# Splitting an FFN activation at half its value, and moving one sigmoid: a sixteen-group transformer-like block on one Trainium2 core

## The chip, the cores and the metric

The kernel runs on one NeuronCore of a Trainium2 chip. Five engines work side by side, each through its own list of instructions in order, and wait for one another on semaphores: TensorE (PE in the rows, its weight loads PEld), VectorE (DVE), ScalarE (ACT), GpSimd (POOL) and SyncE (SP), which only issues transfers here. The metric is the device time of one execution in microseconds (us), lower being better. Kernel before: 286.07 us, median of three runs (285.97 to 286.13).

## The reference, cut to what matters

The input is 32 x 256 rows of 128 numbers. Three layers follow each other, each added to its input:

```
x = x + 0.5 * ffn(layernorm(x))      # first FFN
x = x + rnn(layernorm(x))            # gated recurrence along the 256 steps
x = x + 0.5 * ffn(layernorm(x))      # second FFN, the same weights

ffn(x): h = gelu(ternary_linear(x, w_up))      # 128 -> 512
        return ternary_linear(h, w_down)       # 512 -> 128
ternary_linear(x, w): w_t = sign(w) where |w| > 0.5 * mean|w|, else 0
        rms = sqrt(sum(x*x)) / sqrt(d)
        return (x / (rms + 1e-8)) @ w_t.T
rnn(x): f = sigmoid(x Wf), i = sigmoid(x Wi), c = max(x Wh + 0.5, sigmoid(x Wh))
        hidden_t = f_t * hidden_(t-1) + i_t * c_t,  hidden_0 = 0.5
```

(The recurrence is written in logarithms in the reference; this is what it comes to.) The second linear layer of the FFN divides by the root mean square of h itself, so the kernel needs the sum of squares of each row's 512 values of h, beside h times w_down.

## The kernel before, in words

The 8192 rows stay in SBUF as tensor X, 64 tiles of 128 rows; four tiles are a group, and there are 16 groups. The program passes three times over the groups: 16 steps of the first FFN (F = 0 to 15), 16 steps of the recurrence (r = 0 to 15), 16 steps of the second FFN (F = 16 to 31). Each engine has its own hand-written order of these steps; they overlap only as far as those orders and the semaphores let them.

One step of the FFN, for group F:

- GpSimd normalises the group's four tiles (norm, L213, writes xn) two steps ahead, and turns sums of squares into root mean squares (rms_step, L220 and L224). It also computes the square roots of the layer norms (ln_roots, L187 to L195): in the second FFN one group's roots in each step up to step 11.
- TensorE: up(F, 0) (L405, L406) multiplies the high and low fp16 halves of the transposed input with the ternary weights into PSUM tensor U[0]; turn transposes the next group (L386); up(F, 1) fills U[1]; gram(F-1) (L426, L434) forms h times h-transposed in blocks of 64 rows, whose diagonal holds the sums of squares; down(F-1) (L447) multiplies h with down_w.
- ScalarE: GeLU in place on U[0] (L294), the high half of the next transposed input (xt_hi, L275), h_hi = fp16 of a multiple of the GeLU (L300), the same GeLU and h_hi for U[1], then the diagonal's sums (sum_squares, L326).
- VectorE: the low half of the next input (xt_lo, L563); h_lo (L568), the rest of h that fp16 h_hi doesn't hold, once for U[0] and once for U[1]; then, for the group of two steps ago, y_scale (L583) and the addition into X (L590, four tiles); and layer norm statistics (L546, L552, L626) of groups to come.

up(F, part) waits for h_lo of the same part of group F-1, because both use U[part]. So per step there is one loop through TensorE, ScalarE and VectorE, and each of the four engines also has the sum of its own work.

h is kept as two fp16 tensors. Before, h_hi = fp16(256 h) and h_lo = fp16(256 h - h_hi). The first FFN's gram takes three products, hi x hi, hi x lo and lo x hi, 96 matmuls of 64 columns. The second FFN's gram takes two, hi x (hi/2) and hi x lo, 64 matmuls, for which VectorE writes a third tensor, h_half = h_hi / 2 (h_halves, L578), after each h_lo; gram waits for it.

One step r of the recurrence: TensorE transposes the next group, forms three gates (L462), and transposes the previous hidden state back (L471). ScalarE copies the transposed input (L306), makes sig_h (gate 0), sig_i (gate 1) and the forget gate (gate 2), all on L313, and normalises two of the four tiles of the group after next (norm_tile, L289), one before and one after sig_i. VectorE: scan (L608), candidate (L598, writes cand), statistics, addition (L614). GpSimd: inject = sig_i x cand (L232), then rstd and shift for a coming group (L200, L203), then the other two of the four tiles (L213). norm_tile waits for shift.

The functions that the change touches, and what calls them:

Of the kernel before, what the change touches and what calls it, by code (L numbers as in the profile page):

```python
# [12 lines left out]
P = 128  # L13
TILES = 4
GT = TILES * P
LN_EPS = 1e-5
RMS_EPS = 1e-8
H_SPLIT = 256.0
XN_SPLIT = 4096.0
POOL_TILES = 2  # L20
HALF = P // 2
# [3 lines left out]
def build_macaron(nc, x_in, w_f, w_i, w_h, w_up, w_down, x_out):  # L25
# [12 lines left out]
    with ExitStack() as ctx:  # L38
        def sb(name, shape, dt=F32):
            return ctx.enter_context(nc.sbuf_tensor(name, shape, dt))  # L40

        def sem(name):
            return ctx.enter_context(nc.semaphore(name))
# [31 lines left out]
        xt_lo = sb("xt_lo", [P, 2, GT], F16)  # L75
        h_hi = sb("h_hi", [P, 2, chunks, GT], F16)
        h_lo = sb("h_lo", [P, 2, chunks, GT], F16)
        h_half = sb("h_half", [P, 2, chunks, GT], F16)
        square_junk = sb("square_junk", [P, 2, TILES, P], BF16)
        ssq = sb("ssq", [P, 2, TILES])  # L80
        rms = sb("rms", [P, 2, TILES])
# [35 lines left out]
        shift_done, xn_act_ready = sem("shift_done"), sem("xn_act_ready")  # L117
        xn_ready, xt_ready, xt_taken, hi_ready = sem("xn_ready"), sem("xt_ready"), sem("xt_taken"), sem("hi_ready")
        up_ready, gelu_done = sem("up_ready"), sem("gelu_done")
        h_hi_done, h_lo_done, h_half_done = sem("h_hi_done"), sem("h_lo_done"), sem("h_half_done")  # L120
# [22 lines left out]
        def by_both(n):  # L143
            return groups + 2 <= n < 2 * groups
# [17 lines left out]
        def _(pool):  # L162
# [54 lines left out]
            def rms_step(F):  # L217
                par = F % 2
                pool.wait_ge(ssq_done, F + 1)
                eng.tensor_tensor(rms[:, par, :], ssq[:, par, :], half[:, 0:TILES], ALU.pow).then_inc(rms_ready, 1)  # L220
                pool.wait_ge(rms_ready, F + 1)


                eng.tensor_scalar(rms_den[:, F % 4, :], rms[:, par, :], 2.0 * ((1.0 if F < groups else 2.0) / dff) ** 0.5, 2.0 * H_SPLIT * RMS_EPS,  # L224
                                  ALU.mult, ALU.add).then_inc(rms_den_done, 1)

            def inject_step(g):
# [34 lines left out]
        def _(act):  # L262
# [88 lines left out]
            for r in range(groups):  # L351
                turned(groups + r + 1)
                gate(r, 0)
                if by_both(groups + r + 2):
                    norm_tile(groups + r + 2, 2)
                gate(r, 1)
                if by_both(groups + r + 2):
                    norm_tile(groups + r + 2, 3)
                gate(r, 2)
                if r == 0:  # L360
                    sum_squares(groups - 1)
                if r + 4 < groups:
                    rnn_moments(r + 4)
# [6 lines left out]
        def _(pe):  # L370
# [38 lines left out]
            def gram(F):  # L409

                par = F % 2
                pe.wait_ge(h_lo_done, 2 * F + 2)
                if F >= groups:
                    pe.wait_ge(h_half_done, 2 * (F - groups) + 2)
                if F == 0:
                    pe.wait_ge(consts_set, 5)
                    pe.wait_ge(mask_done, 2)
                    pe.wait_ge(w_taken, 2)  # L420
                elif F == groups:
                    pe.wait_ge(rnn_added, groups)
                if F >= 1:
                    pe.wait_ge(ssq_done, F)
                for n in range(2):
                    pe.matmul(G[n * HALF:(n + 1) * HALF, :, 0:HALF], ident16[:, n * HALF:(n + 1) * HALF], off_diag[:],  # L426
                              start=True, stop=False, tile_position=(0, n * HALF))
                for t in range(TILES):
                    for c in range(chunks):
                        last = t == TILES - 1 and c == chunks - 1  # L430
                        for left, right in ((h_hi, h_hi), (h_hi, h_lo), (h_lo, h_hi)) if F < groups else ((h_hi, h_half), (h_hi, h_lo)):
                            for n in range(2):
                                i = slice(t * P + n * HALF, t * P + (n + 1) * HALF)
                                m = pe.matmul(G[n * HALF:(n + 1) * HALF, t, 0:HALF], left[:, par, c, i], right[:, par, c, i],  # L434
                                              start=False, stop=last and (left is h_lo if F < groups else right is h_lo), tile_position=(0, n * HALF))
                m.then_inc(gram_done, 1)

            def down(F):
                par = F % 2
                if F == 0:  # L440
                    pe.wait_ge(w_taken, 3)
                if F >= 2:
                    pe.wait_ge(ffn_added, F - 1)
                for t in range(TILES):
                    for c in range(chunks):
                        for part in (h_hi, h_lo):
                            m = pe.matmul(Y[:, par, t, :], part[:, par, c, t * P:(t + 1) * P], down_w[:, c, :],  # L447
                                          start=(c == 0 and part is h_hi), stop=(c == chunks - 1 and part is h_lo))
                m.then_inc(down_done, 1)

# [65 lines left out]
        def _(dve):  # L516
# [48 lines left out]

            def h_low(F, part):
                dve.wait_ge(h_hi_done, 2 * F + part + 1)
                vec.scalar_tensor_tensor(out=h_lo[:, F % 2, 2 * part:2 * part + 2, :], in0=U[part][:], scalar=H_SPLIT,  # L568
                                         in1=h_hi[:, F % 2, 2 * part:2 * part + 2, :],
                                         op0=ALU.mult, op1=ALU.subtract).then_inc(h_lo_done, 1)  # L570

            def h_halves(F, part):
                if F < groups:
                    return
                dve.wait_ge(h_hi_done, 2 * F + part + 1)
                if F >= groups + 2:
                    dve.wait_ge(gram_done, F - 1)
                vec.tensor_scalar(h_half[:, F % 2, 2 * part:2 * part + 2, :], h_hi[:, F % 2, 2 * part:2 * part + 2, :],  # L578
                                  0.5, None, ALU.mult).then_inc(h_half_done, 1)

            def scale_y(F):
                dve.wait_ge(rms_den_done, F + 1)
# [73 lines left out]
            for s in range(0, 3 * groups + 2):  # L656
# [48 lines left out]
```

## Time and profile before

| | us |
|---|---|
| time, median of three runs | 286.07 |
| time of the profiled execution | 285.95 |
| its span, first to last instruction | 284.1 |
| outside the span | 1.85 |

| engine | busy us | share of the span |
|---|---|---|
| PE | 249.9 | 88% |
| DVE | 244.6 | 86% |
| ACT | 222.4 | 78% |
| POOL | 220.5 | 78% |

The busy times are sums over the three passes and a start and an end. Which engine holds a pass back is not told by them: for that one reads the chain of waits, stretch by stretch, and the rows of the engines in time order. In a timeline row the first number is the start, the second the length in us; a bracket at the end says how long the engine idled before the row, and what it waited for. Rows of several instructions give the time from the first start to the last end. Instructions of one engine overlap a little, so the distance from start to start is what one costs in a full stretch.

### The profile page before, as it was taken

The page shows a single profiled execution, that of the slowest core. Times are in us where ns is not written, and L with a number is a line of the kernel's source. Part 1 is how long each engine was busy: PE and PEld are TensorE (multiplying, and loading weights), DVE is VectorE, ACT ScalarE, POOL GpSimd, SP SyncE. Part 2 cuts the span into 40 slices and gives each one's busy share as a digit, 9 for nine tenths or more (in the row PEclk, how much of TensorE's full clock was granted, in tenths as well). Part 3 has the DMA queues.
Part 4 walks back from the last instruction along what each step waited for, and adds up shares of the span by engine and source line. Part 5 has one row for each costly group of instructions (what it writes and reads, how often), then busy time and mean ns, then how long its engine had stood idle before and what let it go on. Part 6 is the DMA issues. An engine that isn't in the chain of part 4 may idle for free.

```text
span 284.1 us, 10821 instructions
## 1 busy us (share of the span) xinstructions
PE 249.9 (88%) x4269; PEld 176.1 (62%) x4269; DVE 244.6 (86%) x772; ACT 222.4 (78%) x546; POOL 220.5 (78%) x394
## 2 busy tenths in 40 slices
PE   0568999999999999989999965668999999999973
PEld 0335877878778877735555533336777777667853
DVE  3767699999999898989999946678799999998894
ACT  1267789889898998778888863568999999998971
POOL 4888587878778756579888897898889999899231
PEclk9997999999999999999999999889999999999998
DMA  6990000000000000000000000000021112112213
GB/s 175 278 240 2 3 3 5 2 5 3 2 2 6 2 3 5 3 0 1 3 0 0 0 1 1 2 1 2 2 76 39 42 54 63 40 39 59 59 39 113
DMA packets 18051, 9.81 MB, mean 35 GB/s; under 512 B 592, under 2 KB 17872, under 8 KB 18000
## 3 DMA queue, kind: packets, MB, share of 16 engines
q1 hardware_dynamic: 16896, 8.39, 10.7%
q10 hardware_dynamic: 1104, 0.72, 0.9%
q8 instruction: 34, 0.56, 0.8%
q14 instruction: 17, 0.14, 0.2%
HBM read 4.92 MB, written 4.19 MB: 32 GB/s over the span
## 4 chain that ended last, share of the span: by engine, by line
POOL 38%; PE 37%; DVE 10%; issue 8%; ACT 4%; DMA 1%; POOLq 0%; DVEq 0%; ACTq 0%
PE Y L447 11%; POOL root L192 9%; PE G L434 9%; POOL xn L213 9%; POOL inject L232 6%; PE U L405 6%; PE U L406 5%; POOL rms L220 4%; POOL rstd L200 4%; PE T L386 3%; ACT h_hi L300 2%; ACT U L294 2%; PE G L426 2%; DVE X L590 1%; POOL den L195 1%
## 5 line engine op out<-in xcount | busy, mean ns | idle before, releaser
L294 ACT ACTIVATE U<-U 128x1024 f32<-128x1024 f32 x64 | 65.5, 1024 | 25.0 <-PE U L406 24.8
L568 DVE SCALAR_TENSOR_TENSOR h_lo<-U,h_hi 128x1024 f16<-128x1024 f32 x64 | 77.3, 1218 | 7.3 <-ACT h_hi L300 6.9
L213 POOL TENSOR_SCALAR xn<-X,neg_mean,rstd 128x128 f32<-128x128 f32 x164 | 74.2, 467 | 7.2 <-DVE rstd L559 5.0
L300 ACT ACTIVATE h_hi<-U 128x1024 f16<-128x1024 f32 x64 | 65.7, 1026 | 1.1
L447 PE MATMUL Y<-down_w,h_lo 128*128 128x128 f16 x512 | 60.8, 219 | 0.6 <-issue 0.6
L447 PE MATMUL Y<-down_w,h_hi 128*128 128x128 f16 x512 | 61.2, 220 | 0.0
L405 PE MATMUL U<-xt_hi,up_w 128*128 128x512 f16 x128 | 50.8, 397 | 5.4 <-DVE h_lo L568 4.1
L220 POOL TENSOR_TENSOR rms<-ssq,half 128x4 f32<-128x4 f32 x32 | 32.8, 1024 | 25.2 <-ACT square_junk L326 25.2
L192 POOL TENSOR_TENSOR root<-mv,half 128x8 f32<-128x8 f32 (+1 forms) x26 | 50.5, 1942 | 2.2
L406 PE MATMUL U<-xt_lo,up_w 128*128 128x512 f16 x128 | 50.8, 397 | 0.0
L447 PEld LDWEIGHTS Y<-down_w,h_lo 128*128 128x128 f16 x512 | 50.1, 98 | 0.9 <-issue 0.9
L447 PEld LDWEIGHTS Y<-down_w,h_hi 128*128 128x128 f16 x512 | 49.3, 98 | 1.3
L434 PE MATMUL G<-h_lo,h_hi 128*64 128x64 f16 x1024 | 44.6, 196 | 0.3 <-issue 0.3
L434 PEld LDWEIGHTS G<-h_lo,h_hi 128*64 128x64 f16 x1024 | 41.7, 113 | 0.0
L590 DVE SCALAR_TENSOR_TENSOR X<-Y,y_scale,X 128x128 f32<-128x128 f32 x128 | 36.0, 345 | 1.1
L386 PE MATMUL T<-ident,xn 128*128 128x128 f32 x192 | 31.0, 287 | 2.3 <-POOL xn L213 1.9
L386 PEld LDWEIGHTS T<-ident,xn 128*128 128x128 f32 x192 | 23.8, 148 | 12.9 <-POOL xn L213 4.8
L462 PE MATMUL U<-xt,gate_w 128*128 128x512 f32 x64 | 30.2, 594 | 0.0
L626 DVE BATCH_NORM_STATS2 st<-X 128x6 f32<-128x128 f32 x128 | 29.6, 276 | 0.0
L326 ACT ACTIVATE square_junk<-G 128x64 bf16<-128x64 f32 x128 | 26.7, 230 | 3.1 <-PE G L434 3.1
L232 POOL TENSOR_TENSOR inject<-sig_i,cand 128x512 f32<-128x512 f32 x16 | 20.4, 1274 | 9.2 <-DVE cand L598 6.3
L326 ACT ACTIVATION_READ_ACCUMULATOR square_junk<-G 128x1 f32 x128 | 26.2, 216 | 0.0
(75 smaller groups left out, 482.8 us busy)
## 6 DMA issues: line engine op xcount, KB each, us to landing
X<-in_L_attn_x SPq DMA_DIRECT2D x16, 256.0 KB, 5.2
out_x<-X SPq DMA_DIRECT2D x16, 256.0 KB, 2.5
up_raw<-in_L_ffn_w_up ACTq DMA_DIRECT2D x1, 256.0 KB, 4.1
down_raw<-in_L_ffn_w_down ACTq DMA_DIRECT2D x1, 256.0 KB, 5.0
gate_raw<-in_L_attn_Wh ACTq DMA_DIRECT2D x1, 64.0 KB, 4.5
gate_raw<-in_L_attn_Wi ACTq DMA_DIRECT2D x1, 64.0 KB, 4.3
gate_raw<-in_L_attn_Wf ACTq DMA_DIRECT2D x1, 64.0 KB, 4.2
```

Of the source, the lines that this page charges most:

```text
L192: eng.tensor_tensor(root[l][:, par, 0:w, :], mv[l][:, cols(first, w), 1:3], half[:, 0:2 * w].rearrange("p (t e) -> p t e", e=2), ALU.pow). ...
L213: m = eng.tensor_scalar(xn[:, n % 2, t, :], X[:, c, :], neg_mean[l][:, c:c + 1], rstd[l][:, c:c + 1], ALU.add, ALU.mult)
L220: eng.tensor_tensor(rms[:, par, :], ssq[:, par, :], half[:, 0:TILES], ALU.pow).then_inc(rms_ready, 1)
L294: eng.activation(U[part][:], U[part][:], ACT.Gelu, scale=1.0 / XN_SPLIT).then_inc(gelu_done, 1)
L300: eng.mul(h_hi[:, F % 2, 2 * part:2 * part + 2, :], U[part][:], H_SPLIT).then_inc(h_hi_done, 1)
L326: m = eng.activation(square_junk[:, F % 2, t, 0:HALF], G[:, t, 0:HALF], ACT.Relu, accum_out=ssq[:, F % 2, t:t + 1])
L386: m = pe.transpose(T[:, t * P:(t + 1) * P], xn[:, n % 2, t, :], ident[:])
L405: pe.matmul(U[part][:, c, :], up_w[:, f0:f0 + P], xt_hi[:, F % 2, :], start=True, stop=False)
L406: m = pe.matmul(U[part][:, c, :], up_w[:, f0:f0 + P], xt_lo[:, F % 2, :], start=False, stop=True)
L434: m = pe.matmul(G[n * HALF:(n + 1) * HALF, t, 0:HALF], left[:, par, c, i], right[:, par, c, i], start=False, stop=last and (left is h_lo i ...
L447: m = pe.matmul(Y[:, par, t, :], part[:, par, c, t * P:(t + 1) * P], down_w[:, c, :], start=(c == 0 and part is h_hi), stop=(c == chunks - ...
L568: vec.scalar_tensor_tensor(out=h_lo[:, F % 2, 2 * part:2 * part + 2, :], in0=U[part][:], scalar=H_SPLIT, in1=h_hi[:, F % 2, 2 * part:2 * p ...
```

## The change

Three edits.

- h_hi becomes fp16(h / 2) and h_lo = fp16(h - 2 h_hi). As (h/2)^2 is h_hi^2 + h_hi h_lo but for the square of half the rest, both FFNs' gram takes two products, hi x hi and hi x lo, and h_half and its waits are gone. In return down needs h_hi x w + h_lo x (w/2): a second copy of the weights, down_w_half, is written once by VectorE in step 1, and down(0) waits for it.
- h_lo is written with its operands the other way round: first operand h_hi (fp16, SBUF), second U (fp32, PSUM).
- In the recurrence ScalarE makes sig_i before both tiles that it normalises, not between them.

```diff
-H_SPLIT = 256.0
+H_SPLIT = 0.5
...
             for r in range(groups):
                 turned(groups + r + 1)
                 gate(r, 0)
+                gate(r, 1)
                 if by_both(groups + r + 2):
                     norm_tile(groups + r + 2, 2)
-                gate(r, 1)
-                if by_both(groups + r + 2):
                     norm_tile(groups + r + 2, 3)
                 gate(r, 2)
...
                 pe.wait_ge(h_lo_done, 2 * F + 2)
-                if F >= groups:
-                    pe.wait_ge(h_half_done, 2 * (F - groups) + 2)
...
-                        for left, right in ((h_hi, h_hi), (h_hi, h_lo), (h_lo, h_hi)) if F < groups else ((h_hi, h_half), (h_hi, h_lo)):
+                        for right in (h_hi, h_lo):
...
             def down(F):
                 par = F % 2
                 if F == 0:
-                    pe.wait_ge(w_taken, 3)
+                    pe.wait_ge(w_halved, 1)
...
-                        for part in (h_hi, h_lo):
-                            m = pe.matmul(Y[:, par, t, :], part[:, par, c, t * P:(t + 1) * P], down_w[:, c, :],
+                        for part, w in ((h_hi, down_w), (h_lo, down_w_half)):
+                            m = pe.matmul(Y[:, par, t, :], part[:, par, c, t * P:(t + 1) * P], w[:, c, :],
...
-                vec.scalar_tensor_tensor(out=h_lo[:, F % 2, 2 * part:2 * part + 2, :], in0=U[part][:], scalar=H_SPLIT,
-                                         in1=h_hi[:, F % 2, 2 * part:2 * part + 2, :],
-                                         op0=ALU.mult, op1=ALU.subtract).then_inc(h_lo_done, 1)
...
-                vec.tensor_scalar(h_half[:, F % 2, 2 * part:2 * part + 2, :], h_hi[:, F % 2, 2 * part:2 * part + 2, :],
-                                  0.5, None, ALU.mult).then_inc(h_half_done, 1)
+                vec.scalar_tensor_tensor(out=h_lo[:, F % 2, 2 * part:2 * part + 2, :], in0=h_hi[:, F % 2, 2 * part:2 * part + 2, :],
+                                         scalar=-1.0 / H_SPLIT, in1=U[part][:], op0=ALU.mult, op1=ALU.add).then_inc(h_lo_done, 1)
+
+            def halve_down():
+                dve.wait_ge(w_taken, 3)
+                vec.tensor_scalar(down_w_half[:], down_w[:], H_SPLIT, None, ALU.mult).then_inc(w_halved, 1)
...
                         low_part(F + 1)
+                    if F == 1:
+                        halve_down()
                     h_low(F, 0)
-                    h_halves(F, 0)
                     h_low(F, 1)
-                    h_halves(F, 1)
```

VectorE in one step of the second FFN, before (U01 and U23 are U[0] and U[1]):

```order
L563 SCALAR_TENSOR_TENSOR xt_lo<-T,xt_hi 128x512
L568 SCALAR_TENSOR_TENSOR h_lo<-U01,h_hi 128x1024
L578 TENSOR_SCALAR h_half<-h_hi 128x1024
L568 SCALAR_TENSOR_TENSOR h_lo<-U23,h_hi 128x1024
L578 TENSOR_SCALAR h_half<-h_hi 128x1024
L583 RECIPROCAL y_scale<-rms_den 128x4
L590 SCALAR_TENSOR_TENSOR X<-Y,y_scale,X 128x128 x4
```

and now:

```order
L559 SCALAR_TENSOR_TENSOR xt_lo<-T,xt_hi 128x512
L564 SCALAR_TENSOR_TENSOR h_lo<-h_hi,U01 128x1024
L564 SCALAR_TENSOR_TENSOR h_lo<-h_hi,U23 128x1024
L573 RECIPROCAL y_scale<-rms_den 128x4
L580 SCALAR_TENSOR_TENSOR X<-Y,y_scale,X 128x128 x4
```

Both h_half are gone, and the two h_lo stand together, as they did in the first FFN.

ScalarE in one step of the recurrence, before (the forget gate is written over Y, its own input):

```order
L306 COPY xt<-T 128x512
L313 ACTIVATE sig_h<-U23 128x512
L289 ACTIVATE xn<-X,shift,rstd1 128x128
L313 ACTIVATE sig_i<-Y 128x512
L289 ACTIVATE xn<-X,shift,rstd1 128x128
L313 ACTIVATE Y<-Y 128x512
L281 ACTIVATE var_eps<-mv1 128x4
L282 ACTIVATE neg_mean1<-mv1 128x4
```

and now:

```order
L305 COPY xt<-T 128x512
L312 ACTIVATE sig_h<-U23 128x512
L312 ACTIVATE sig_i<-Y 128x512
L288 ACTIVATE xn<-X,shift,rstd1 128x128 x2
L312 ACTIVATE Y<-Y 128x512
L280 ACTIVATE var_eps<-mv1 128x4
L281 ACTIVATE neg_mean1<-mv1 128x4
```

sig_i stands one place earlier, ahead of the first xn and of that instruction's wait for shift.

VectorE in step 1 of the first FFN now, where the halved weights are made:

```order
L555 RECIPROCAL rstd0<-den0 128x4
L542 BN_STATS st<-X 128x6 x4
L548 BN_AGGR mv0<-st 128x2 x4
L559 SCALAR_TENSOR_TENSOR xt_lo<-T,xt_hi 128x512
L569 TENSOR_SCALAR down_w_half<-down_w 128x512
L564 SCALAR_TENSOR_TENSOR h_lo<-h_hi,U01 128x1024
L564 SCALAR_TENSOR_TENSOR h_lo<-h_hi,U23 128x1024
```

The new instruction is the fifth row; the others stood in this order before.

## Rows read from the trace of the kernel before

**Rows 1.** The chain of waits: start us, length us, work; first FFN, then second FFN

```profile
...
30.65 0.44 PE T L386 x4
...
32.18 1.52 PE G L434 x96
...
36.46 0.44 PE T L386 x4
...
261.58 1.01 PE G L434 x64
...
```

**Rows 2.** Timeline of DVE in the first FFN; start us, length us

```profile
...
35.12 1.22 DVE L568 SCALAR_TENSOR_TENSOR h_lo<-U,h_hi 128x1024 f16<-128x1024 f32 x1 [0.75 <-ACT h_hi L300]
...
40.93 1.22 DVE L568 SCALAR_TENSOR_TENSOR h_lo<-U,h_hi 128x1024 f16<-128x1024 f32 x1 [0.44 <-ACT h_hi L300]
...
47.87 0.17 DVE L583 RECIPROCAL y_scale<-rms_den 128x4 f32<-128x4 f32 x1
...
89.69 0.17 DVE L583 RECIPROCAL y_scale<-rms_den 128x4 f32<-128x4 f32 x1
...
94.29 1.23 DVE L568 SCALAR_TENSOR_TENSOR h_lo<-U,h_hi 128x1024 f16<-128x1024 f32 x1 [0.75 <-ACT h_hi L300]
...
112.25 1.22 DVE L568 SCALAR_TENSOR_TENSOR h_lo<-U,h_hi 128x1024 f16<-128x1024 f32 x1 [0.61 <-ACT h_hi L300]
```

**Rows 3.** Timeline of POOL in the recurrence

```profile
...
137.56 0.20 POOL L203 TENSOR_TENSOR shift<-neg_mean,rstd 128x4 f32<-128x4 f32 x1
...
138.91 1.27 POOL L232 TENSOR_TENSOR inject<-sig_i,cand 128x512 f32<-128x512 f32 x1 [0.29 <-issue]
...
142.57 1.27 POOL L232 TENSOR_TENSOR inject<-sig_i,cand 128x512 f32<-128x512 f32 x1 [0.29 <-issue]
```

**Rows 4.** Timeline of ACT in the same step

```profile
...
137.12 0.60 ACT L313 ACTIVATE sig_h<-U 128x512 f32<-128x512 f32 x1 [0.27 <-PE U L462]
137.80 0.49 ACT L289 ACTIVATE xn<-X,shift,rstd 128x128 f32<-128x128 f32 x1
138.20 0.58 ACT L313 ACTIVATE sig_i<-Y 128x512 f32<-128x512 f32 x1
...
```

**Rows 5.** Timeline of DVE in two steps of the recurrence

```profile
...
125.03 0.67 DVE L614 TENSOR_TENSOR X<-G,X 128x512 f32<-128x512 f32 x1
125.62 1.26 DVE L608 TENSOR_TENSOR_SCAN hidden<-Y,inject 128x256 f32<-128x256 f32 x2
...
139.53 0.68 DVE L614 TENSOR_TENSOR X<-G,X 128x512 f32<-128x512 f32 x1
140.22 1.27 DVE L608 TENSOR_TENSOR_SCAN hidden<-Y,inject 128x256 f32<-128x256 f32 x2
...
```

**Rows 6.** Timeline of POOL in the second FFN

```profile
...
203.51 1.01 POOL L220 TENSOR_TENSOR rms<-ssq,half 128x4 f32<-128x4 f32 x1 [0.70 <-ACT square_junk L326]
...
204.90 1.75 POOL L213 TENSOR_SCALAR xn<-X,neg_mean,rstd 128x128 f32<-128x128 f32 x4
...
209.18 1.01 POOL L220 TENSOR_TENSOR rms<-ssq,half 128x4 f32<-128x4 f32 x1
...
256.37 1.01 POOL L220 TENSOR_TENSOR rms<-ssq,half 128x4 f32<-128x4 f32 x1
...
257.76 2.01 POOL L213 TENSOR_SCALAR xn<-X,neg_mean,rstd 128x128 f32<-128x128 f32 x4
...
```

**Rows 7.** Timeline of DVE under the last of these

```profile
...
258.26 0.41 DVE L578 TENSOR_SCALAR h_half<-h_hi 128x1024 f16<-128x1024 f16 x1
...
```

**Rows 8.** The chain of waits at the end of the second FFN

```profile
...
275.89 0.43 DVE h_half L578
...
```

**Rows 9.** Groups of instructions by line and form: busy us, mean ns | idle before

```profile
...
L568 DVE SCALAR_TENSOR_TENSOR h_lo<-U,h_hi 128x1024 f16<-128x1024 f32 x64 | 77.3, 1218 | 7.3 <-ACT h_hi L300 6.9
...
L578 DVE TENSOR_SCALAR h_half<-h_hi 128x1024 f16<-128x1024 f16 x32 | 13.4, 419 | 0.0
...
L540 DVE SCALAR_TENSOR_TENSOR down_t<-down_raw,limit,below 128x512 f32<-128x512 f32 x1 | 0.8, 821 | 0.0
...
```

More of the change, by code:

```diff
@@ L61, in build_macaron @@
         down_w = sb("down_w", [P, chunks, d], F16)
+        down_w_half = sb("down_w_half", [P, chunks, d], F16)
         gate_w = sb("gate_w", [P, 3, d])
@@ L77, in build_macaron @@
         h_lo = sb("h_lo", [P, 2, chunks, GT], F16)
-        h_half = sb("h_half", [P, 2, chunks, GT], F16)
         square_junk = sb("square_junk", [P, 2, TILES, P], BF16)
@@ L119, in build_macaron @@
         up_ready, gelu_done = sem("up_ready"), sem("gelu_done")
-        h_hi_done, h_lo_done, h_half_done = sem("h_hi_done"), sem("h_lo_done"), sem("h_half_done")
+        h_hi_done, h_lo_done, w_halved = sem("h_hi_done"), sem("h_lo_done"), sem("w_halved")
         gram_done, ssq_done, rms_ready = sem("gram_done"), sem("ssq_done"), sem("rms_ready")
@@ L221, in rms_step @@
                 pool.wait_ge(rms_ready, F + 1)
-                eng.tensor_scalar(rms_den[:, F % 4, :], rms[:, par, :], 2.0 * ((1.0 if F < groups else 2.0) / dff) ** 0.5, 2.0 * H_SPLIT * RMS_EPS,
+                eng.tensor_scalar(rms_den[:, F % 4, :], rms[:, par, :], 2.0 / dff ** 0.5, 2.0 * H_SPLIT * RMS_EPS,
                                   ALU.mult, ALU.add).then_inc(rms_den_done, 1)
@@ L430, in gram @@
                         last = t == TILES - 1 and c == chunks - 1
-                        for left, right in ((h_hi, h_hi), (h_hi, h_lo), (h_lo, h_hi)) if F < groups else ((h_hi, h_half), (h_hi, h_lo)):
+                        for right in (h_hi, h_lo):
                             for n in range(2):
                                 i = slice(t * P + n * HALF, t * P + (n + 1) * HALF)
-                                m = pe.matmul(G[n * HALF:(n + 1) * HALF, t, 0:HALF], left[:, par, c, i], right[:, par, c, i],
-                                              start=False, stop=last and (left is h_lo if F < groups else right is h_lo), tile_position=(0, n * HALF))
+                                m = pe.matmul(G[n * HALF:(n + 1) * HALF, t, 0:HALF], h_hi[:, par, c, i], right[:, par, c, i],
+                                              start=False, stop=last and right is h_lo, tile_position=(0, n * HALF))
                 m.then_inc(gram_done, 1)
@@ L567, in h_low @@
                 dve.wait_ge(h_hi_done, 2 * F + part + 1)
-                vec.scalar_tensor_tensor(out=h_lo[:, F % 2, 2 * part:2 * part + 2, :], in0=U[part][:], scalar=H_SPLIT,
-                                         in1=h_hi[:, F % 2, 2 * part:2 * part + 2, :],
-                                         op0=ALU.mult, op1=ALU.subtract).then_inc(h_lo_done, 1)
[L572 to L577, printed above, removed]
-                vec.tensor_scalar(h_half[:, F % 2, 2 * part:2 * part + 2, :], h_hi[:, F % 2, 2 * part:2 * part + 2, :],
-                                  0.5, None, ALU.mult).then_inc(h_half_done, 1)
+                vec.scalar_tensor_tensor(out=h_lo[:, F % 2, 2 * part:2 * part + 2, :], in0=h_hi[:, F % 2, 2 * part:2 * part + 2, :],
[3 more added lines that the diff above has]
+                vec.tensor_scalar(down_w_half[:], down_w[:], H_SPLIT, None, ALU.mult).then_inc(w_halved, 1)
             def scale_y(F):
```

## The prediction

> **What bounds the kernel now.** I read the chain of waits first, because four engines are 78 to 88% busy and the sums don't say which one holds a pass back. The reader is to see that its steps change engine. In the first FFN the chain runs along TensorE alone: one step is the distance between two transposes, 36.46 - 30.65 = 5.81 us, and 96 gram matmuls take 1.52 of it, while 64 of them take 1.01 in the second FFN [rows 1]. But the timeline of VectorE beside it shows that TensorE is not alone at its limit. VectorE idles before an h_lo in the first steps, 0.75 and 0.44 us; then from 47.87 to 89.69, seven steps of 5.97 us, it is full, and it idles again before the h_lo of 94.29 and 112.25 [rows 2]. 5.97 is more than TensorE's 5.81: from step 4 on VectorE is the bound, since from step 3 on it has statistics of two layers to make.
>
> In the recurrence a step is 3.66 us (138.91 to 142.57) [rows 3]. GpSimd's inject sits idle 0.29 before it starts, put down to "issue", which names nothing. The timeline of ScalarE names it: sig_i ends at 138.20 + 0.58 = 138.78, and inject starts 0.13 later. Going back, sig_i starts when the first xn has run, and that xn, at 137.80, starts when shift ends on GpSimd (137.56 + 0.20 = 137.76), 0.68 after sig_h started instead of the usual 0.48 [rows 3, 4]. So the loop is inject, rstd, shift, xn on ScalarE, sig_i, inject.
>
> In the second FFN GpSimd never idles from 203.51 to 259.77. Its undisturbed step is 209.18 - 203.51 = 5.67, yet nine steps take 256.37 - 203.51 = 52.86, or 5.87 each, and the four xn of 1.75 take 2.01 at 257.76, where VectorE runs an h_half at 258.26 [rows 6, 7]. I looked through the stretched GpSimd instructions between, and each lies over an h_half.
>
> **The change, part by part.** All against the profiled execution, 285.95 = 284.1 of span + 1.85 around it; the median is 286.07, 0.12 above it.
>
> *Gram of the first FFN.* 32 of 96 matmuls go: 1.52 - 1.01 = 0.51 us per step of TensorE [rows 1]. Where it counts is read from VectorE. Two grams, 0 and 1, end before the GeLUs that feed the h_lo at 40.93, so that one comes 2 x 0.51 = 1.02 earlier; VectorE's idle before it, 0.75 + 0.44 = 1.19 in these rows, leaves room for that [rows 2]. From there VectorE is full at 5.97 per step and the other 0.51s buy nothing while it is. At 94.29 there is 0.75 of idle and at 112.25 there is 0.61 [rows 2]. Before the first, the up matmuls are held soon after by h_lo of the group before, so between 0 and 0.51 comes back; I take 0.3. Before the second, TensorE by then has gained more than 0.61, so all of it: 0.61. Together 1.02 + 0.3 + 0.61 = 1.9. Bounds: 1.0 (the first term alone) and 15 x 0.51 = 7.7 (TensorE alone the bound), of which VectorE's idle admits 0.75 + 0.44 + 0.75 + 0.61 = 2.6.
>
> *down_w_half.* One VectorE operation of 512 fp16 values. No row shows this size; between a reciprocal of 4 values, 0.17, and h_half of 1024, 0.42 [rows 2, 9], I take 0.3. It is queued ahead of h_lo of group 1, which waits for ScalarE anyway, and down(0) comes after the first gram, about 1.5 us later. Cost 0, with cover; without the cover 0.3 once.
>
> *h_lo with turned operands.* 64 operations of 1.218. The nearest other row of this kind with both tensors in SBUF is down_t, 0.821 for 512 values, twice that being 1.64 [rows 9]. On the other side stands h_half, 0.419 for the same 1024 values with one operand [rows 9]. Between 0.42 and 1.64 I take 1.218, the same operation on the same two memories.
>
> The Trainium skill, "VectorE: DVE Perf Modes", section "The perf-mode tier table", has any operand in PSUM hold a two-tensor operation at one element per cycle; by that rule the order of the operands is indifferent, and the sum is unchanged; no run before shows the turned order.
>
> *sig_i ahead.* sig_i is released 0.40 (the first xn) + 0.20 (the wait for shift) earlier. What is late next? GpSimd's own step: 3.66 less the 0.29 of idle = 3.37. ScalarE's: 3.66 less the 0.20 stall = 3.46. VectorE's is the largest: its addition at 139.53 is followed by the scan 0.69 later, because the scan waits for inject (138.91 + 1.27 = 140.18); unforced the distance is 125.62 - 125.03 = 0.59, so VectorE's own step is 3.66 - 0.10 = 3.56 [rows 3 to 5]. The step falls by 0.10, not 0.29. It repeats ten times: 1.0. At the end, where the chain leaves VectorE for the square roots on GpSimd, inject keeps its shorter wait: 0.2 more. Together 1.2; bounds 0 and 10 x 0.20 + 0.2 = 2.2 (ScalarE's 3.46 as the floor). The xn now waiting behind sig_i end no later than before, since the second one stood behind sig_i already.
>
> *h_half gone.* VectorE loses 32 x 0.419 = 13.4 us [rows 9]. Nearly all of it lies under GpSimd's full stretch and buys nothing by itself. Three places count. At the start of the second FFN, both h_half of group 16 stand between the last scan and the last addition, for which gram(16) waits: 0.84, less some 0.1 that one of them hides in a wait for ScalarE: 0.7. In GpSimd's stretch the overlaps go: 52.86 - 9 x 5.67 = 1.83, and 2.01 - 1.75 = 0.26 on the last xn: 2.1 [rows 6]. At the end the last h_half stands alone on the chain: 0.43 [rows 8]. Sum 3.2. Bounds: 1.1 (if GpSimd's stretching has another cause) and 3.8, adding what a little slack in the two steps before 203.51 (idle 0.70) may give.
>
> The trace shows GpSimd stretched by 0 to 0.35 us per step where it meets an h_half [rows 6, 7]. The Trainium skill, "SBUF — State Buffer", section "SBUF: two separate sides", calls the port that both engines share an exclusive lock held for a whole instruction, with the other blocked fully. By that, read literally, up to 2 x 0.419 per step would be GpSimd waiting, 7.5 us over nine steps, four times the 1.83 measured; the measurement decides.
>
> Sum: 1.9 + 1.2 + 3.2 = 6.3. 285.95 - 6.3 = 279.65, about 279.6.
>
> **The rivals.**
> - *More comes back.* VectorE's distances contain waits of its own that shrink, so that the recurrence goes at ScalarE's 3.46 (1.0 more) and the first FFN gives the whole 2.6 (0.7 more). For it: both full engines there are full of short operations. Against: VectorE shows no idle in seven steps of rows 2. Time 285.95 - 8.0 = 277.9.
> - *GpSimd's stretching is not h_half's.* Then 2.1 is not gained: 281.7. For it: many h_half overlap GpSimd operations that are not stretched. Against: no stretched one lies elsewhere.
> - *The moved sigmoid does nothing*, because the two xn behind it now release the next transpose later, or because the addition and the scan on VectorE keep their distance: 1.2 is lost, 280.9.
> - *The turned operands are slower.* Each h_lo on VectorE costs x more. In the first FFN, full on VectorE, 13 steps x 2 x x are on the path; in the second its step is at most 5.87 - 0.84 = 5.03 without h_half, which leaves 5.67 - 5.03 = 0.64 of slack, so x stays out there up to 0.32. It decides from 26 x = 6.3, x = 0.24 on. At the upper bound, x = 1.64 - 1.22 = 0.42, it costs 26 x 0.42 = 10.9 and in nine steps of the second FFN 0.84 - 0.64 = 0.2 each, 1.8: 292.4, slower than before. For it: no row has this order. Against: 1.64 comes from a row that reads no PSUM, and the new order reads the same two memories as the old.
>
> **How the numbers follow.** Forecast 0.60 (own range 278.4 to 280.8), more comes back 0.10, GpSimd's stretch stays 0.12, sigmoid nothing 0.12, turned operands decide 0.04, the rest 0.02 for a change that comes out even by several of these. The range 277.7 to 282.2 takes in the first four with their spread and leaves out about 0.15. A measurement of this kernel can tell some 0.2% from no change. Faster 0.94, same 0.02, slower 0.04.
>
> **What would show it.** First FFN: 64 gram matmuls in 1.0, VectorE still at 5.9 to 6.0 per step in its middle, h_lo at 40.93 now near 39.9. Recurrence: steps of 3.56, VectorE without a gap, inject within 0.1 of cand's end. Second FFN: GpSimd at 5.67 in every step, no xn of 2.0, VectorE idle by about 0.6 per step. h_lo at 1.22. It would be wrong if h_lo has another length, if GpSimd's step stays at 5.87, or if the recurrence stays at 3.66.

## The result: 283.15 us against 286.1, where 279.6 was forecast

The changed kernel takes 283.15 us (median of 4 runs, 283.00 to 284.11), the kernel before 286.1 beside it (4 runs, 285.97 to 287.41). The ratio is 0.9894, with a 95% interval of 0.9858 to 0.993. It is faster, but by 3.0 and not by 6.3. The profiled execution of the changed kernel took 283.0: a span of 281.3 and 1.7 around it.

Three events cut both executions into the same pieces: the start of the first inject, that of the last inject, and that of the last rms, all on GpSimd.

| piece | before | after | difference | forecast |
|---|---|---|---|---|
| start to the first inject (first FFN) | 118.20 | 115.96 | -2.24 | -1.9 |
| first to last inject (recurrence) | 65.42 | 67.12 | +1.70 | -1.2 |
| last inject to last rms (second FFN) | 95.14 | 92.83 | -2.31 | -3.2 with the end |
| the rest and what lies around the span | 7.19 | 7.09 | -0.10 | 0 |

The recurrence is 2.9 off and holds most of the miss; the second FFN falls 0.9 short as well, and the first gives 0.3 more than was forecast.

**First FFN.** The timeline of VectorE, rows of h_lo and y_scale (start, length, and in brackets the idle time before and its releaser):

```profile
34.35 1.22 DVE L564 SCALAR_TENSOR_TENSOR h_lo<-h_hi,U 128x1024 f16<-128x1024 f16 x1 [0.75 <-ACT h_hi L299]
...
38.50 2.36 DVE L564 SCALAR_TENSOR_TENSOR h_lo<-h_hi,U 128x1024 f16<-128x1024 f16 x2
...
46.52 0.17 DVE L573 RECIPROCAL y_scale<-rms_den 128x4 f32<-128x4 f32 x1
...
70.10 0.17 DVE L573 RECIPROCAL y_scale<-rms_den 128x4 f32<-128x4 f32 x1
...
92.55 1.22 DVE L564 SCALAR_TENSOR_TENSOR h_lo<-h_hi,U 128x1024 f16<-128x1024 f16 x1 [0.75 <-ACT h_hi L299]
```

Two h_lo run back to back from 38.50, so the second starts at about 39.7, where 40.93 stood [rows 2]: the idle of 0.44 is gone, and the text said "near 39.9". From 46.52 to 70.10 there are four steps without idle, two of 6.05 and two of 5.74, 5.90 on average. In the kernel before, the same stretch was not quite full: an h_lo there waited for ScalarE, and from 59.67 to 71.84 the two steps took 12.17, not 11.79.

```profile
64.90 1.23 DVE L568 SCALAR_TENSOR_TENSOR h_lo<-U,h_hi 128x1024 f16<-128x1024 f32 x1 [0.22 <-ACT h_hi L300]
...
71.84 0.17 DVE L583 RECIPROCAL y_scale<-rms_den 128x4 f32<-128x4 f32 x1
```

In the changed kernel TensorE now waits for VectorE, as its own timeline says:

```profile
63.47 0.38 PE L403 MATMUL U<-xt_hi,up_w 128*128 128x512 f16 x1 [0.60 <-DVE h_lo L564]
...
69.20 0.38 PE L403 MATMUL U<-xt_hi,up_w 128*128 128x512 f16 x1 [0.28 <-DVE h_lo L564]
```

**Recurrence.** A step was 3.66 [rows 3]; now it is 3.84. One step on four engines, from the timeline:

```profile
133.31 1.27 POOL L231 TENSOR_TENSOR inject<-sig_i,cand 128x512 f32<-128x512 f32 x1 [0.47 <-DVE cand L588]
...
135.57 0.60 ACT L312 ACTIVATE sig_h<-U 128x512 f32<-128x512 f32 x1 [0.28 <-PE U L458]
135.63 0.20 POOL L203 TENSOR_TENSOR shift<-neg_mean,rstd 128x4 f32<-128x4 f32 x1
...
136.19 0.69 DVE L588 SCALAR_TENSOR_TENSOR cand<-U,sig_h 128x512 f32<-128x512 f32 x1 [0.20 <-ACT sig_h L312]
...
136.42 0.60 ACT L312 ACTIVATE sig_i<-Y 128x512 f32<-128x512 f32 x1 [0.26 <-PE Y L458]
...
136.92 0.87 ACT L288 ACTIVATE xn<-X,shift,rstd 128x128 f32<-128x128 f32 x2
...
137.16 1.27 POOL L231 TENSOR_TENSOR inject<-sig_i,cand 128x512 f32<-128x512 f32 x1 [0.47 <-DVE cand L588]
...
137.88 0.63 PE L384 MATMUL T<-ident,xn 128*128 128x128 f32 x4 [0.20 <-issue]
```

The sigmoid got its place ahead of both xn and found nothing to read: it idles 0.26 for gate 1's matmul and starts 0.85 after sig_h. Both xn stand behind it, so the second ends at 137.79, 2.22 after sig_h started. Neither waits for its shift, which ends on GpSimd at 135.83, 1.09 before the first of them. Before, the first xn stood in the gap between the two gates' matmuls, and the second ended 2.03 after sig_h (0.68 + 0.40 + 0.95) [rows 4]. The next transpose on TensorE follows 0.09 behind the second xn. The chain of waits (start, length, work) has moved from GpSimd to TensorE accordingly:

```profile
133.84 0.20 issue
134.04 0.63 PE T L384 x4
134.67 0.86 PE U L458 x2
135.53 1.72 PE Y L458 x4
137.25 0.44 PE G L467 x4
137.68 0.20 issue
137.88 0.63 PE T L384 x4
```

The ring is transpose, gates 0 and 1, sig_i, two xn, transpose: 1.53 from the transpose to sig_h, 0.85 to sig_i, 0.50 to the first xn, 0.87 for both, 0.09 to the transpose: 3.84.

**Second FFN.** GpSimd's timeline:

```profile
203.36 1.01 POOL L220 TENSOR_TENSOR rms<-ssq,half 128x4 f32<-128x4 f32 x1 [0.29 <-ACT square_junk L325]
...
209.01 1.01 POOL L220 TENSOR_TENSOR rms<-ssq,half 128x4 f32<-128x4 f32 x1
...
254.17 1.01 POOL L220 TENSOR_TENSOR rms<-ssq,half 128x4 f32<-128x4 f32 x1
...
258.67 1.73 POOL L213 TENSOR_SCALAR xn<-X,neg_mean,rstd 128x128 f32<-128x128 f32 x4
```

Nine steps take 50.81, or 5.65 each, where 5.87 stood; no four xn take longer than 1.74, where one took 2.01 [rows 6]. The groups (busy us, mean ns) answer to [rows 9]:

```profile
L564 DVE SCALAR_TENSOR_TENSOR h_lo<-h_hi,U 128x1024 f16<-128x1024 f16 x64 | 76.9, 1216 | 12.8 <-ACT h_hi L299 12.6
...
L569 DVE TENSOR_SCALAR down_w_half<-down_w 128x512 f16<-128x512 f16 x1 | 0.3, 283 | 0.0
```

But the stretch begins late. Windows of 2 us on TensorE (window, its length, busy and matmuls, granted clock, DMA share, GB/s):

```profile
186.00:188.00 2.00, 1.37 (x6) 0.88 0.02 4
188.00:190.00 2.00, 0.66 (x4) 0.98 0.00 0
190.00:192.00 2.00, 1.82 (x5) 0.50 0.00 0
192.00:194.00 2.00, 2.00 (x11) 0.67 0.00 0
```

From 190 to about 193.3 the granted clock is at its half level, 1.2 GHz, behind 1.34 of idle from 188 to 190, just as the first full burst of up matmuls comes: they stand 0.42 to 0.43 apart until 193.12 and 0.21 apart from 193.44. Before, the clock stood at 1.00 from 188 on. So although the last inject starts 0.54 earlier, gram 16 starts only 0.15 earlier, at 193.96 instead of 194.11.

### The profile page after: what moved, and what is told of

Same layout as the page of the kernel before. It is cut to its first block, busy times and chain, and to the rows that moved or that the text cites. A ratio compares the mean times of both kernels' runs of the same rounds, so it can differ in the third digit from the quotient of the medians.

```text
span 281.3 us, 9737 instructions
## 1 busy us (share of the span) xinstructions
PE 242.9 (86%) x3757; PEld 168.6 (60%) x3757; DVE 234.8 (83%) x741; ACT 222.4 (79%) x546; POOL 217.1 (77%) x394
## 4 chain that ended last, share of the span: by engine, by line
PE 46%; DVE 29%; POOL 10%; issue 8%; ACT 6%; DMA 1%; POOLq 0%; DVEq 0%; ACTq 0%
PE Y L443 10%; DVE h_lo L564 7%; PE U L458 6%; PE U L403 6%; DVE X L580 6%; PE G L430 6%; PE U L404 6%; PE T L384 5%; POOL root L192 4%; PE Y L458 3%; DVE st L542 3%; DVE xt_lo L559 3%; DVE mv L548 3%; ACT h_hi L299 3%; DVE st L616 3%
## 5 line engine op out<-in xcount | busy, mean ns | idle before, releaser
L564 DVE SCALAR_TENSOR_TENSOR h_lo<-h_hi,U 128x1024 f16<-128x1024 f16 x64 | 76.9, 1216 | 12.8 <-ACT h_hi L299 12.6
L213 POOL TENSOR_SCALAR xn<-X,neg_mean,rstd 128x128 f32<-128x128 f32 x164 | 72.2, 453 | 6.4 <-DVE rstd L555 4.1
L443 PE MATMUL Y<-down_w_half,h_lo 128*128 128x128 f16 x512 | 60.6, 219 | 0.0
L403 PE MATMUL U<-xt_hi,up_w 128*128 128x512 f16 x128 | 51.4, 402 | 10.0 <-DVE h_lo L564 8.5
L443 PEld LDWEIGHTS Y<-down_w_half,h_lo 128*128 128x128 f16 x512 | 50.1, 98 | 0.0
L430 PE MATMUL G<-h_lo,h_hi 128*64 128x64 f16 x1024 | 36.8, 196 | 0.0
L430 PE MATMUL G<-h_hi 128*64 128x64 f16 x1024 | 36.8, 196 | 0.0
L430 PEld LDWEIGHTS G<-h_hi 128*64 128x64 f16 x1024 | 35.8, 113 | 0.0
L384 PE MATMUL T<-ident,xn 128*128 128x128 f32 x192 | 31.6, 290 | 3.5 <-issue 2.2
L430 PEld LDWEIGHTS G<-h_lo,h_hi 128*64 128x64 f16 x1024 | 34.1, 113 | 0.0
```

Of the source, the lines that this page charges most:

```text
L213: m = eng.tensor_scalar(xn[:, n % 2, t, :], X[:, c, :], neg_mean[l][:, c:c + 1], rstd[l][:, c:c + 1], ALU.add, ALU.mult)
L384: m = pe.transpose(T[:, t * P:(t + 1) * P], xn[:, n % 2, t, :], ident[:])
L403: pe.matmul(U[part][:, c, :], up_w[:, f0:f0 + P], xt_hi[:, F % 2, :], start=True, stop=False)
L430: m = pe.matmul(G[n * HALF:(n + 1) * HALF, t, 0:HALF], h_hi[:, par, c, i], right[:, par, c, i], start=False, stop=last and right is h_lo, ...
```

## The experiments

Twelve further sets of runs follow, in three batches of four; each batch shares one chip with 17 runs of the kernel before (medians 285.89, 286.16, 285.93). One program's executions spread over 1.4 to 4.2 us, and part of that goes with the granted clock: of the 17 of the first batch, the four with a mean granted clock of 0.99 took 283.66 to 285.62, the thirteen with 0.973 to 0.981 took 285.32 to 287.51. So besides medians and ratios I compare pieces of the traces.

| run | median (range, n) | ratio to before [95%] | recurrence | last inject to last rms |
|---|---|---|---|---|
| e1 split only | 282.26 (280.35-284.02, 6) | 0.9865 [0.9814, 0.9915] | 65.40 | 93.88 |
| e2 sigmoid only | 287.9 (285.29-288.8, 12) | 1.0064 [1.0033, 1.0094] | 67.17 | 95.71 |
| e3 split, clock | 281.58 (280.38-281.81, 6) | 0.9833 [0.9794, 0.9872] | 65.38 | 93.20 |
| e4 no h_half | 282.58 (281.77-284.6, 6) | 0.9892 [0.9845, 0.9939] | 65.37 | 91.90 |
| e5 gram of two | 284.28 (282.85-286.5, 12) | 0.994 [0.9906, 0.9974] | 65.30 | 94.71 |
| e6 operands back | 283.26 (280.89-284.71, 6) | 0.9898 [0.9847, 0.9949] | 67.13 | 91.64 |
| e7 scales early | 279.6 (277.79-281.09, 6) | 0.9778 [0.973, 0.9827] | 62.50 | 93.57 |
| e8 scales, clock | 278.95 (277.83-279.29, 6) | 0.9751 [0.9705, 0.9798] | 62.56 | 91.90 |
| e9 warm start | 277.41 (276.12-278.53, 6) | 0.971 [0.9658, 0.9761] | 62.58 | 91.91 |
| ea scales early, sigmoid ahead | 282.22 (280.72-282.87, 6) | 0.9869 [0.9824, 0.9914] | 65.93 | 93.91 |
| a2 changed kernel again | 283.1 (280.72-284.6, 12) | 0.9899 [0.9866, 0.9932] | 67.18 | 93.22 |
| e1b split only again | 282.19 (281.53-283.82, 6) | 0.9877 [0.9832, 0.9922] | 65.40 | 93.76 |

**e1: the split alone**, ScalarE's order as before.

```diff
                 gate(r, 0)
-                gate(r, 1)
                 if by_both(groups + r + 2):
                     norm_tile(groups + r + 2, 2)
+                gate(r, 1)
```

> The changed kernel with ScalarE's order of the recurrence as before (xn, sig_i, xn). Theory G (the moved sigmoid is released by gate 1's matmul, not by the xn, so it holds both xn and then TensorE's next transpose): the step goes from 3.84 back to 3.66, ten to eleven steps, 1.9 us faster than the changed kernel: about 281.2. Theory V (the recurrence slowed for another reason, such as the split): no change, 283.1.

The step is 3.66 again (ten steps 36.66) and the recurrence 1.72 shorter than in the changed kernel. Of that, 1.05 comes back in the second FFN, where this trace has half clock from about 187 to 193.6. The medians differ by 0.9 only, half of the 1.9 that was expected.

**e2: the sigmoid alone**, on the kernel before: the edit of e1 the other way round.

> The kernel before with the sigmoid moved alone. Theory G: step 3.84, 10 x 0.18 slower: about 287.9. The prediction on record said 1.2 faster, 284.9. Theory V: no change, 286.1.

Ten steps take 38.45, and the kernel is slower by 0.64% (interval 0.33 to 0.94%), 1.8 us. The moved sigmoid is a loss in itself, with or without the split.

**e3: e1 with throwaway matmuls** before the last turn backs, which keep TensorE busy and whose result nobody reads.

```diff
             def turn_back(g):
-                pe.wait_ge(scan_done, g + 1)
...
+                for _ in range({12: 24, 13: 18, 14: 18, 15: 10}.get(g, 0)):
+                    pe.matmul(O[:, :, 0:HALF], ident16[:], off_diag[:], start=True, stop=True)
+                pe.wait_ge(scan_done, g + 1)
```

> e1_split_only with throwaway matmuls (bf16, 64 x 4 columns wide, into the PSUM tensor that the transpose back overwrites) in TensorE's four waits of 1.1 to 3 us at the end of the recurrence: 24, 18, 18 and 10 of them at about 0.11 us. Theory C (the granted clock of 0.5 between 182 and 194 is due to TensorE's idling there, and costs the second FFN about 1.2 us at its start): granted clock 1.00 throughout 180 to 200, gram(16) about 1.2 us earlier, total 1.0 to 1.5 below e1. Rival D (the start is held by GpSimd's roots and VectorE's last addition): same as e1, within 0.3.

The clock is 1.00 in every window up to 188, in e1 up to 186, and then it still falls (0.70 from 188 to 190, 0.50 from 190 to 192). TensorE's last two idles before that:

```profile
186.56 0.66 PE L470 MATMUL G<-ident,hidden 128*128 128x128 f32 x4 [1.31 <-DVE hidden L601]
...
188.36 0.38 PE L404 MATMUL U<-xt_hi,up_w 128*128 128x512 f16 x1 [1.14 <-DVE h_lo L567]
```

The piece is 0.68 shorter and the median 0.68 lower, where 1.0 to 1.5 was expected; the intervals of e1 and e3 overlap.

**e4: the kernel before without h_half**; VectorE's instruction and the waits for it go with it.

```diff
-... else ((h_hi, h_half), (h_hi, h_lo)):
+... else ((h_hi, h_hi), (h_hi, h_lo)):
```

> The kernel before without h_half; the second FFN's gram multiplies h_hi with h_hi and h_lo (this leaves out the halving, so its sums of squares are too large). It isolates the third term of the prediction: 3.2 faster, 282.9, if TensorE's clock recovers where it did before; about 2.0 to 2.3 faster, 284, if the clock is low for longer as in the changed kernel. GpSimd's step 5.65 in both. Rival: the stretching of GpSimd has another cause, its step stays 5.87, and the gain is 1.1: 285.0.

The last piece falls from 95.14 to 91.90, by 3.24, with GpSimd's steps at 5.67; the forecast's term was 3.2. Its parts come out too: 0.74 up to the rms of group 17 (0.7 was forecast), 1.87 in the nine steps behind it (1.83) and 0.63 in the rest (0.26 + 0.43). In this trace the clock is 1.00 from 186 on.

**e5: 64 gram matmuls in the first FFN** of the kernel before: the products of h_hi with h_hi and with h_lo remain.

```diff
-... ((h_hi, h_hi), (h_hi, h_lo), (h_lo, h_hi)) if F < groups ...
+... ((h_hi, h_hi), (h_hi, h_lo)) if F < groups ...
```

> The kernel before with 64 instead of 96 gram matmuls in the first FFN (the product lo x hi is left out there, so its sums of squares lack that part). It isolates the first term: the prediction said 1.9, the changed kernel's trace shows 2.2 by the first addition of the recurrence: about 284.0. Rival (TensorE alone bounds the first FFN): 15 x 0.51 = 7.7 faster, 278.4.

The first inject starts at 116.11, 2.09 earlier than in the profile before and 1.3 to 1.4 earlier than in e2 and e4; the ratio says 0.6% or 1.7 us.

**e6: the changed kernel with h_lo's operands turned back.**

```diff
-... in0=h_hi[...], scalar=-1.0 / H_SPLIT, in1=U[part][:], op0=ALU.mult, op1=ALU.add)
+... in0=U[part][:], scalar=H_SPLIT, in1=h_hi[...], op0=ALU.mult, op1=ALU.subtract)
```

> The changed kernel with h_lo computed from U first and h_hi second, as before (h/2 - h_hi instead of h - 2 h_hi, so the rest enters at half its weight). Theory: the order is indifferent, 1.22 us each, total 283.1 within 0.3. Rival: the turned order is cheaper or dearer: at 0.1 each, 2.6 in the first FFN.

The group of h_lo in its profile:

```profile
L564 DVE SCALAR_TENSOR_TENSOR h_lo<-U,h_hi 128x1024 f16<-128x1024 f32 x64 | 77.1, 1219 | 12.4 <-ACT h_hi L299 12.3
```

1219 against 1216 ns, so the order is indifferent here; the medians, of two batches, are 283.26 and 283.15. Its profiled execution took 280.89, with a clock of 1.00 from 186 on and the last piece at 91.64.

**e7: e1 with GpSimd's rstd and shift issued one group earlier**, so that no xn waits for a shift of its own step.

```diff
-                if 0 <= s - 13 < groups:
-                    rnn_scales(s - 13)
+                for g in {13: (0,), 14: (1,), 15: (2, 3)}.get(s, (s - 12,) if 16 <= s < groups + 12 else ()):
+                    rnn_scales(g)
```

> e1_split_only with GpSimd's rstd and shift one group earlier throughout the recurrence (two groups in step 15 of the first FFN, then one per step). Theory: the loop inject, rstd, shift, xn, sig_i, inject is cut, as shift is there a step ahead; then xn stands in the wait between sig_h and gate 1's matmul, sig_i follows it, and the step falls from 3.66 to VectorE's own 3.56: 1.0 faster than e1, 280.2. Rival: another wait holds 3.66 (TensorE's transposes after the second xn), or GpSimd is late at the start of the recurrence: same or slower than e1.

The step falls to 3.47 and, when VectorE has filled up, to 3.53; the recurrence is 2.90 shorter than in e1, where 1.0 was expected. Of that, 1.6 comes from ten steps and 1.26 from the step between the inject of groups 12 and 13 (7.18 in e1, 5.92 here), which the expectation had left out. The kernel is 2.66 faster by the medians, which are of two batches; the ratios, 0.9778 and 0.9865, say 2.5.

**e8: e7 with the throwaway matmuls of e3.**

> e7 with the throwaway matmuls of e3. If both theories hold their gains add: about 279.0. If neither holds, as e1.

The median is 278.95, as expected. Here the clock is 1.00 in every window of the start of the second FFN:

```profile
186.00:188.00 2.00, 2.00 (x12) 1.00 0.04 8
188.00:190.00 2.00, 1.85 (x75) 1.00 0.00 0
```

But the matmuls are those of e3, and so are TensorE's last two idles:

```profile
184.10 0.66 PE L470 MATMUL G<-ident,hidden 128*128 128x128 f32 x4 [1.32 <-DVE hidden L601]
...
185.90 0.38 PE L404 MATMUL U<-xt_hi,up_w 128*128 128x512 f16 x1 [1.14 <-DVE h_lo L567]
```

So what the matmuls leave uncovered doesn't explain why the clock fell in e3's trace; that stays open. Over all executions the matmuls do raise the mean granted clock: 0.972 to 0.979 in e1 and 0.990 to 1.000 in e3, 0.972 to 0.988 in e7 and 0.989 to 0.994 here (the means take in the whole kernel, its start too). The last piece is 91.90 against e7's 93.57. The gain in time is smaller than that 1.67: the mean of the six runs falls by 0.97 from e1 to e3 and by 0.92 from e7 to e8, together 0.95 with a 95% interval of about 0.2 to 1.7. The chain in the recurrence shows TensorE alone and without issue time, so 3.47 is the sum of TensorE's own work:

```profile
132.92 0.44 PE G L470 x4
133.36 0.46 PE T L385 x4
133.82 0.86 PE U L459 x2
134.68 1.72 PE Y L459 x4
136.39 0.44 PE G L470 x4
```

**e9: e8 with more throwaway matmuls**, at the kernel's start as well. The conditions around the nine are left out here.

```diff
-            pe.wait_ge(consts_set, 4)
+            pe.wait_ge(consts_set, 5)
+            pe.wait_ge(mask_done, 2)
+            for _ in range(20):
+                pe.matmul(U01[:, 0, 0:2 * P], ident16[:], off_diag[:], start=True, stop=True)
...
+                        for _ in range(9 if F == 1 else 0):
+                            pe.matmul(G[:, :, 0:HALF], ident16[:], off_diag[:], start=True, stop=True)
...
-                for _ in range({12: 24, 13: 18, 14: 18, 15: 10}.get(g, 0)):
+                for _ in range({12: 24, 13: 18, 14: 18, 15: 22}.get(g, 0)):
```

> The version with GpSimd's scales one group earlier and with throwaway matmuls around the third pass (e8), with more throwaway matmuls: 20 of 256 columns on TensorE before its first matmul of the kernel, 9 before the second group of the first FFN, and 22 instead of 10 after the last turn back. The output's computation is unchanged. Theory one, the half-rate matmuls of the first 25 us (512 columns 0.43 apart) hold the first FFN's start: with TensorE at 2.4 GHz from about 20 us on, the first step is shorter, inject(0) comes 0.7 to 1.5 earlier than in e8 (116.22, so 114.7 to 115.5) and the time is 277.5 to 278.3. Theory two, the start is held by GpSimd's roots and VectorE's statistics, or VectorE's full step of 5.9 takes the gain back: inject(0) within 0.4 of 116.2 and 278.9, as e8. The second FFN from inject(15) to the last rms is 91.9 in both.

TensorE's timeline, the up matmuls behind the transpose of about 23 us, e8's first, then e9's:

```profile
23.86 0.63 PE L404 MATMUL U<-xt_hi,up_w 128*128 128x512 f16 x1
24.28 0.63 PE L405 MATMUL U<-xt_lo,up_w 128*128 128x512 f16 x1
```

```profile
23.62 0.38 PE L412 MATMUL U<-xt_hi,up_w 128*128 128x512 f16 x1
23.83 0.38 PE L413 MATMUL U<-xt_lo,up_w 128*128 128x512 f16 x1
```

0.42 apart in e8, 0.21 in e9: 1.2 GHz against 2.4 GHz. The first inject comes at 114.99 instead of 116.22 and the last piece is as in e8. One other trace has the full rate here, e6, which has none of these matmuls: its eight up matmuls from 22.42 to 24.37 stand 0.21 to 0.22 apart within each four. From the first up matmul to the first inject e6 takes 101.02 and e9 101.03; the other nine traces with 64 gram matmuls, all with half rate in part of this stretch, take 102.27 to 103.47. So full rate here goes with a gain of at least 1.2. That the added matmuls brought it in e9 is not shown, as e6 had it without them. The up matmuls of 14 to 16 us are still 0.43 apart in e9, in spite of the twenty in front of them. The medians, 277.41 and 278.95, are of two batches and their ratios' intervals overlap. This is the version with the lowest median.

**ea: the changed kernel with the scales one group earlier.**

> The changed kernel (the sigmoid of the input gate ahead of both xn), with GpSimd's rstd and shift issued one group earlier. Theory G, the recurrence's step is held by TensorE's loop (transpose, both gates' matmuls, sig_i, two xn, next transpose): the step stays 3.84, although shift is no longer in it, and only the end of the recurrence gets shorter, by about 1.26 as in e7 against e1; time 283.1 - 1.3 = 281.8. Rival, the step of 3.845 comes from shift ending late on GpSimd ahead of the two xn: with the scales early the step falls to 3.5 and the time to 278.5 to 280.

Ten steps take 38.46. ScalarE and GpSimd in one of them:

```profile
135.44 0.60 ACT L312 ACTIVATE sig_h<-U 128x512 f32<-128x512 f32 x1 [0.28 <-PE U L458]
...
135.69 0.20 POOL L203 TENSOR_TENSOR shift<-neg_mean,rstd 128x4 f32<-128x4 f32 x1
...
136.30 0.60 ACT L312 ACTIVATE sig_i<-Y 128x512 f32<-128x512 f32 x1 [0.26 <-PE Y L458]
...
136.79 0.87 ACT L288 ACTIVATE xn<-X,shift,rstd 128x128 f32<-128x128 f32 x2
```

No xn here can wait for a shift of its own step, and the step is 3.85 all the same; under the old order the same edit took it to 3.5. The rival is out: gate 1's matmul holds the ring through sig_i and the two xn behind it. Only the end of the recurrence gets shorter, by 1.2.

**a2 and e1b: the changed kernel and the split alone, on one chip.**

> The changed kernel again, for more executions beside the one with ScalarE's old order on the same chip. Theory G: the step of 3.845 against 3.66 costs 10 x 0.185 = 1.85, less what the end of the recurrence gives back, so 1.5 to 1.9 above e1b. Rival, the later end of the recurrence is taken back by the second FFN: within 0.5 of e1b.

> The activation split and its gram and h_half changes alone, with ScalarE's order as before the change, on the same chip as the changed kernel. Theory G: 281.3 to 281.6 where the changed kernel has 283.1. Rival: equal within 0.5.

The step is as expected in both, 3.84 and 3.67, but the medians are 283.1 and 282.19, not 1.5 to 1.9 apart. All 16 runs of the changed kernel have a mean of 283.04, all 12 of the split alone 282.30: 0.74 apart, with a 95% interval of about 0.0 to 1.5. Both of my expectations for the total were off. In the traces the recurrence costs 1.78, and 0.54 (a2 and e1b) to 1.05 (after and e1) comes back behind it: the split alone reaches the second FFN earlier and meets half clock from about 186 to 193 there. Windows of e1b:

```profile
186.00:188.00 2.00, 1.12 (x4) 0.54 0.02 4
188.00:190.00 2.00, 1.68 (x5) 0.50 0.00 0
190.00:192.00 2.00, 2.00 (x8) 0.50 0.00 0
192.00:194.00 2.00, 2.00 (x68) 0.76 0.00 0
```

## Why the prediction was wrong in size

**The step that failed** is the sentence "The xn now waiting behind sig_i end no later than before, since the second one stood behind sig_i already". It asked when sig_i is free to start on ScalarE and not whether its input is there. The moved sigmoid waits for gate 1's matmul, 0.85 behind gate 0's, and the gap that the first xn had filled stays empty; then two xn run where one ran. The forecast had summed each engine's own work (GpSimd 3.37, ScalarE 3.46, VectorE 3.56), not TensorE's, which is 3.47 (e8), and not this ring through TensorE and ScalarE, which closes at 3.84. Expected 1.2 saved, measured 1.70 lost: 2.9 of the 3.4 that the forecast is off. The second FFN adds 0.9, and the first FFN and the rest take 0.4 back. The rival "the moved sigmoid does nothing" named just this path (the next transpose released later) but priced it at nothing; the lower bound of the term, 0, had no reason that excluded a loss. e2 shows the loss alone, e1 its absence, and ea and e7 together show that it isn't the shift.

**The ring of GpSimd was read rightly.** Inject, rstd, shift, xn, sig_i held the step at 3.66: with the shift early and the old order (e7) it goes to 3.47, then 3.53, VectorE's own step, which the text had put at 3.56.

**First FFN, 1.9.** The difference of the two profiles is 2.24. The start varies between executions: the first inject stands at 118.20, 117.52 and 117.44 in the three profiles with 96 matmuls per gram (before, e2, e4), and at 116.11 on average in the ten with 64 and the old start, which are all but e9 (115.03 to 117.19). That makes 1.6. The mechanism held, VectorE's full stretch taking most of the 7.7 back, and 1.9 lies between the two readings. Its terms came out unevenly. Compared at VectorE's y_scale of the same group, the changed kernel is 1.35 ahead at 46.52 (1.02 was forecast; part of it is the different start). It is 1.74 ahead at 70.10, because the stretch that the prediction called full of work held the idle of 0.22 at 64.90 and two slower steps. It is still 1.74 ahead at 105.48: the idle of 0.75 that stood at 94.29 is there again at 92.55, so the term of 0.3 brought nothing. At 111.15 it is 2.24 ahead (0.61 forecast, 0.50 measured). In this execution the sum was right in part by luck.

**h_half, 3.2.** e4 measures 3.24. The changed kernel shows 2.31, and the part that is missing is the one at the start: the forecast had 0.7 saved up to the rms of group 17, and the changed kernel comes there 0.39 later than before (20.28 from the last inject, against 19.89), because half clock covers its up matmuls. So 1.1 is lost there, and 0.2 comes back in the steps behind. The undisturbed length of the whole piece is 91.9 (e4, e8 and e9; 91.64 in e6, where GpSimd's steps are 5.65 as in the changed kernel and not 5.67), the changed kernel has 92.83 and 93.22, the split alone 93.76 and 93.88. I had not looked at the granted clock after 184, though removing h_half and moving the last inject were bound to shift what TensorE does there. The Trainium skill, "TensorE: Matmul & The Clock Gate", section "What's actually happening", has the array throttled by default and its activity release the throttle. This case agrees in e8, where with throwaway matmuls the clock stays at 1.00 through the transition and the piece is 1.67 shorter than in e7; e3, with the same matmuls, fell to half clock all the same.

GpSimd's stretching by VectorE's h_half is gone in the changed kernel, 50.81 for nine steps against 52.86: 2.05, where 1.83 was taken and e4 measures 1.87.

**The terms at nothing.** down_w_half took 0.283 (0.3 said) and h_lo 1.216 (1.218 said).

Sum of the profiled pieces: -2.24 + 1.70 - 2.31 - 0.10 = -2.95, the 285.95 - 283.0 that was measured.

**What stays open.** Which stretch of half clock an execution gets is not decided by the code alone (e6 and the changed kernel differ in nothing that matters, 91.64 against 92.83; e3 and e8 have the same matmuls and the same last idles). Nor is it chance alone: the mean granted clock is 0.972 to 0.979 in all 12 executions of the split alone and 0.979 to 0.990 in all 16 of the changed kernel, though e6 has 0.972 to 0.990. No run here separates the two, so how much of an early arrival comes back can only be given as a spread.

## What to carry to other kernels

An instruction moved ahead in an engine's order starts early only if its input is early too; look up when the producer ends before moving it, and what work filled the gap until then, because that work is now late. Price each ring through the new order, with the wait for the producer in it, and take the largest; the loss side of such a term is the ring's, not zero. Where a pass ends with TensorE idling for one to two microseconds at a time, the next pass may begin at half clock, in one execution and not in another; throwaway matmuls in those waits brought about 0.95 us here. Look at the clock in windows at such a place before you count on a gain ahead of it.

## What the hardware showed that I had not expected

- Near the kernel's start e8's matmuls of 512 columns are 0.42 to 0.43 apart as late as 25 us, half the rate that they have later. The two traces with full rate from 22 us on (e6 and e9) reach the first inject 1.2 to 2.5 us sooner after the first up matmul than the others with 64 gram matmuls.
- From 14 to 16 us the same matmuls are 0.40 to 0.43 apart in every trace, and in e7's from 22.5 to 26 as well, while the windows give a granted clock of 1.00 there: near the start the distance between matmuls tells the rate, and the clock row does not.
- A gain ahead of such a transition is partly returned by it: 1.72 to 1.78 us less recurrence gave 0.9 us in the medians and 0.7 in the means.
- The mean granted clocks of the changed kernel and of the kernel before are alike (0.982 and 0.984), though from 190 to 194 the kernel before has 1.00 and the changed kernel 0.50 and 0.67: of one execution the mean says little, the windows at the transition say it.
